# Group 0 of a DLRM tower in two halves: its columns made by TensorE from masked embeddings, its shifted rows copied at once, and W2 turned wholly inside the loop

## What is computed

```python
def _cin_layer(X0, Xi, W, b):          # X0: B x 39 x 16, Xi: B x Fi x 16
    Wr = W.reshape(H, F0_, Fi)         # H = 128
    return jnp.einsum('hjk,bjd,bkd->bhd', Wr, X0, Xi) + b[None, :, None]
...
for W, b in Ws:                        # W0, W1, W2
    Xi = _cin_layer(X0, Xi, W, b)
    res.append(Xi.sum(axis=2))         # z: 512 x 384
h = jnp.maximum(concat([z, dense_ctx]) @ W_top1 + b_top1, 0.0)
h = jnp.maximum(h @ W_top2 + b_top2, 0.0)
y = h @ W_top3
```

## Time and profile before

| what | value |
|---|---|
| median of 3 runs | 670.46 us (669.49 to 670.49) |
| profiled execution, first to last instruction | 667.2 us |
| around the span, by the median | 3.3 us |
| TensorE busy | 642.2 us (96%) |
| VectorE, ScalarE, GpSimd busy | 572.6, 561.4, 358.9 us |
| first layer 1 matmul | at 40.48 us |

### The profile page before, as it was taken

How to read it: one execution, slowest core, us unless ns; L and a number is a source line. 1 busy time by engine, 2 the same in 40 slices (tenths; PEclk the granted TensorE clock), 3 DMA queues, 4 the chain that set the end, 5 groups by cost and what they waited for, 6 DMA issues and landing times.

```text
span 667.2 us, 11319 instructions
## 1 busy us (share of the span) xinstructions
PE 642.2 (96%) x2662; PEld 482.4 (72%) x2662; DVE 572.6 (86%) x894; ACT 561.4 (84%) x1941; POOL 358.9 (54%) x394
## 2 busy tenths in 40 slices
PE   3899999999999999999999999999999999999998
PEld 2667677777777777777777777777777777777874
DVE  3568888989898989899898989898989989899890
ACT  2558889889898989898888889898989898899773
POOL 7648863837565574747383847556474315142700
PEclk9899999999999999999999999999999999999999
DMA  8245614133240505141413324150504140110000
GB/s 292 22 83 130 122 13 104 22 68 58 41 86 13 107 9 114 10 110 15 106 18 74 50 46 79 18 105 7 116 8 112 10 106 6 43 44 1 1 1 0
DMA packets 67523, 39.52 MB, mean 59 GB/s; under 512 B 58791, under 2 KB 61863, under 8 KB 65349
## 3 DMA queue, kind: packets, MB, share of 16 engines
q1 hardware_dynamic: 60463, 37.71, 25.3%
q0 software_dynamic: 5120, 1.29, 2.6%
q10 hardware_dynamic: 1904, 0.15, 0.2%
HBM read 32.80 MB, written 2.40 MB: 53 GB/s over the span
## 4 chain that ended last, share of the span: by engine, by line
PE 82%; DVE 7%; ACT 5%; issue 4%; DMA 2%; DVEq 0%; ACTq 0%; SPq 0%; POOLq 0%
PE yb L992 19%; PE yb L996 18%; PE yb L993 18%; PE p L958 13%; PE pq L969 5%; DVE acc L816 3%; ACT yb L634 3%; DMA gram<-in_L_rec_W_dram 2%; DVE x L822 2%; DVE yb L800 1%; PE yb L1109 1%; PE pq L923 1%; PE p L1054 1%; PE p L1086 1%; PE p L1084 1%
## 5 line engine op out<-in xcount | busy, mean ns | idle before, releaser
L634 ACT ACTIVATE yb<-yb,x0t 128x128 f32<-128x128 f32 x1728 | 467.4, 369 | 57.5 <-PE yb L996 52.5
L816 DVE TENSOR_TENSOR acc<-acc,yb 128x512 f32<-128x512 f32 (+1 forms) x512 | 323.4, 668 | 32.5 <-ACT yb L634 32.2
L992 PE MATMUL yb<-w1h,x1h 128*128 128x512 f32 (+1 forms) x640 | 307.8, 481 | 6.9 <-DVE acc L816 6.0
L996 PE MATMUL yb<-w1h,x1l 128*128 128x512 f32 (+1 forms) x640 | 247.5, 387 | 0.0
L993 PE MATMUL yb<-w1l,x1h 128*128 128x512 f32 (+1 forms) x640 | 247.2, 386 | 0.0
L427 POOL DMA_INDIRECT emb<-in_table_dram,idx x160 | 152.6, 954 | 44.8 <-issue 38.9
L485 POOL TENSOR_TENSOR late<-late,x0r 117x512 f32<-117x512 f32 (+1 forms) x105 | 132.5, 1297 | 79.6 <-DMA late<-x_scratch 79.4
L992 PEld LDWEIGHTS yb<-w1h,x1h 128*128 128x128 f32 x640 | 120.2, 188 | 62.9 <-DVE acc L816 25.1
L993 PEld LDWEIGHTS yb<-w1l,x1h 128*128 128x128 f32 x640 | 120.6, 188 | 45.8 <-issue 24.7
L996 PEld LDWEIGHTS yb<-w1h,x1l 128*128 128x128 f32 x640 | 120.1, 188 | 25.0 <-DVE x1l L771 0.4
L474 POOL TENSOR_TENSOR bdiag<-mask,x0t 128x312 f32<-128x312 f32 x64 | 45.5, 711 | 142.2 <-PE pq L969 138.9
(11 more groups left out here) (108 smaller groups left out, 317.8 us busy)
## 6 DMA issues: line engine op xcount, KB each, us to landing
late<-x_scratch SPq DMA_DIRECT2D x45, 312.0 KB
late<-x_scratch SPq DMA_DIRECT2D x30, 234.0 KB
emb<-in_table_dram,idx POOLq DMA_INDIRECT x160
gram<-in_L_rec_W_dram SPq DMA_DIRECT2D x1, 2496.0 KB, 11.0
x_scratch<-x0r SPq DMA_DIRECT2D x15, 156.0 KB
late<-x_scratch SPq DMA_DIRECT2D x15, 156.0 KB
w2t<-in_L_rec_W_dram SPq DMA_DIRECT2D x1, 1280.0 KB, 14.5
x0t<-embt SPq DMA_DIRECT2D x64, 20.0 KB
```

Of the source, the lines that this page charges most:

```text
L634: op = act.activation(part, part, ACT.Copy, scale=x0t[u][:, t, j:j + 1])
L816: dve.tensor_tensor(part, part, parts(y_bank(t, m), n), ALU.add).then_inc(summed, 1)
L992: pe.matmul(y[:, 0:w], hi, w1h[:, at:at + w], start=True, stop=False)
L996: pe.matmul(y[:, 0:w], lo, w1h[:, at:at + w], start=False, stop=True).then_inc(bank_ready, 1)
```

## The change

Group 0's 32 samples go through the head in two halves of 16 (tiles 0 and 1, tiles 2 and 3). The ids and table offsets are loaded so that one gather brings two fields' columns for 16 samples; the first half needs 5 gathers and not 10. VectorE widens each gathered block by a mask (`widen`), and TensorE makes the columns from it with 10 small matmuls (`half_px`), in the place of `dims_outside`, `samples`, `columns` and `three_times` for this group. ScalarE copies all shifted rows in two instructions (`half_shifts`). VectorE makes W0 symmetric in 4 larger instructions and does pairs in 4. The `WARM` turns are gone. W1 comes in two DMAs. The second half's columns, turns, shifts, pairs and `layer0` are placed in tiles 0 and 1 of period 0. Fields of group 1 are turned at (2, 2) of period 0, of group 2 at (0, 6) and of group 3 at (3, 6) of period 1; layer 0 of group 1 runs from (3, 3) to (3, 9) of period 0, that of group 2 from (1, 9) to (3, 2) of period 1. All ten banks of W2 are turned in the loop. The rows in the DRAM scratch are read with a stride of three rows.

```diff
-FIRST_LAYER0_SLOTS = ((1, 8), (2, 0), (2, 2), (2, 5), (2, 8), (3, 1), (3, 4))
-NEXT_TURN_SLOT, NEXT_COPY_SLOT = (0, 0), (0, 0)
-W2_FIRST = 5
-W2_SLOTS = ((4, 6), (4, 9), (5, 6), (5, 9), (6, 9))
+PX_SLOT, HALF_TURN_SLOT = (0, 5), (0, 8)
+HALF_THREE_SLOT, HALF_COPY_SLOT = (0, 7), (0, 9)
+HALF_SHIFT_SLOTS = ((1, 0), (1, 2), (1, 4), (1, 6))
+HALF_LAYER0_SLOTS = {(1, 3): (0, 1), (1, 5): (2, 3), (1, 7): (4, 5), (1, 8): (6,)}
+HALF_HIGH_SLOT = (1, 9)
+SPREAD_AT, HALF_LOW_AT = (0, ("sum", 1)), (1, ("sum", 7))
+HALF_PAIRS_AT = (("scale", 0), ("sum", 1), ("sum", 4), ("fold before", 0))
+THREE_SLOTS = {0: {(2, 1): 1}, 1: {(0, 4): 2, (3, 0): 3}}
+TURN_SLOTS = {0: {(2, 2): 1}, 1: {(0, 6): 2, (3, 6): 3}}
+COPY_SLOTS = {0: {(2, 2): 1}, 1: {(0, 7): 2, (3, 7): 3}}
+EARLY_LAYER0 = {0: {(3, 3): (0,), (3, 5): (1,), (3, 6): (2,), (3, 8): (3,), (3, 9): (4, 5, 6)},
+                1: {(1, 9): (0,), (2, 1): (1,), (2, 3): (2,), (2, 5): (3,), (2, 8): (4,), (3, 0): (5,), (3, 2): (6,)}}
+HIGH_SLOTS = {0: (3, 9)}
+W2_SLOTS = ((3, 6), (4, 1), (4, 9), (5, 1), (5, 6), (5, 9), (6, 1), (6, 6), (6, 9), (7, 1))
-WARM = 24
...
-                        first = x0d[u, c0 + CHUNKS * q:c0 + CHUNKS * q + FIELDS, :]
+                        first = x0d[u, REPS * c0 + q:REPS * c0 + q + FIELDS, :]
-                        src = bass.AP(first.tensor, first.offset, [[row, FIELDS], [row, n], [1, GROUP_N]])
+                        src = bass.AP(first.tensor, first.offset, [[row, FIELDS], [REPS * row, n], [1, GROUP_N]])
...
+            def half_columns(h):
+                px = pq[:, 0:HALF_T * COLS].rearrange("p (t c) -> p t c", t=HALF_T)
+                tiles = slice(h * HALF_T, (h + 1) * HALF_T)
+                act.wait_ge(px_done, h + 1)
+                act.activation(x0t3[:, tiles, :].rearrange("p t (r j) -> p t r j", r=REPS),
+                               px[:, :, None, 0:FIELDS].to_broadcast([P, HALF_T, REPS, FIELDS]),
+                               ACT.Copy).then_inc(half_x0t3_ready, 1)
+                act.activation(x0t[0][:, tiles, :], px, ACT.Copy).then_inc(half_x0t_ready, 1)
...
+            def half_px(h):
+                if h > 0:
+                    pe.wait_ge(half_x0r_ready, h)
+                for k in range(HALF_K):
+                    pe.wait_ge(wide_ready, h * HALF_K + k + 1)
+                    for t in range(HALF_T):
+                        px = pq[:, t * COLS:(t + 1) * COLS].rearrange("p (q i k) -> p k i q", i=HALF_I, k=HALF_K)
+                        op = pe.matmul(px[:, k], wide[h][:, k, t * P:(t + 1) * P],
+                                       mask[:, :].rearrange("p (i q) -> p i q", i=HALF_I), start=True, stop=True)
+                op.then_inc(px_done, 1)
...
+            for n in range(W0_BANKS):            # TensorE's head
+                turn_w0(n)
+            half_px(0)
+            for b in range(4):
+                turn_w1(b)
+            half_turn(0)
+            half_shift(0, 0)
+            half_shift(0, 1)
+            turn_order = {1: 2, 3: 3}
             for c in range(CHUNKS):
-                layer0(0, c)
+                half_layer0(0, c)
+                if c in turn_order:
+                    half_shift(0, turn_order[c])
+            for b in range(4, W_BANKS):
+                turn_w1(b)
...
             for n in range(W0_BANKS):            # ScalarE's head
+                copy_w0(n)
+            copy_w1(0)
+            half_columns(0)
+            half_shifts(0, 0, 2)
+            half_fields(0)
+            half_shifts(0, 2, CHUNKS)
+            for b in range(1, 4):
+                copy_w1(b)
...
+            half_high(0)
+            for b in range(4, W_BANKS):
+                copy_w1(b)
...
+            for k in range(HALF_K):              # VectorE's head, behind W0
+                widen(k)
+            for b in range(4):
+                low_w1(b)
+            for s in range(DOUBLES):
+                half_products(0, s)
+            low_w1(4)
+            half_low(0)
+            for b in range(5, W_BANKS):
+                low_w1(b)
```

More of the change, by code:

```diff
@@ L199, in tower @@
         w0_in = sem("w0_in")
-        w1_in = sem("w1_in")
+        w1_in = [sem(f"w1_in{h}") for h in range(len(W1_PIECES) - 1)]
         w2_in = [sem(f"w2_in{h}") for h in range(len(W2_PIECES) - 1)]
@@ new lines, in half_shifts @@
+            def half_shifts(h, c0, c1):
+                act.wait_ge(half_x0t3_ready, h + 1)
+                first = x0t3[:, h * HALF_T:(h + 1) * HALF_T, REPS * c0:REPS * c0 + FIELDS]
+                part, tiles, cols = first.ap
+                n = min(REPS * c1, SHIFTS) - REPS * c0
+                act.activation(shifted[h][:, :, REPS * c0 * FIELDS:(REPS * c0 + n) * FIELDS].rearrange("p t (r j) -> p t r j", r=n),
+                               bass.AP(first.tensor, first.offset, [part, tiles, [1, n], cols]),
+                               ACT.Copy).then_inc(half_shifts_ready, 1)
@@ new lines, in half_turn, with half_shift @@
+            def half_turn(h):
+                pe.wait_ge(half_x0t3_ready, h + 1)
+                pe.wait_ge(half_x0t_ready, h + 1)
+                for t in range(HALF_T):
+                    op = pe.transpose(pq[0:ROWS, t * P:(t + 1) * P], x0t3[:, h * HALF_T + t, :], ident[:, :])
+                op.then_inc(half_turned, 1)
+            def half_shift(h, s):
+                if h == 0:
+                    head_bank_free("shift", s)
+                elif s == 0:
+                    pe.wait_ge(x0r_ready, 1)
+                else:
+                    pe.wait_ge(pairs_ready, 2 * s)
+                y = head_bank("shift", s) if h == 0 else pq
+                pe.wait_ge(half_shifts_ready, 2 * h + (1 if s == 0 else 2))
+                for n, c in enumerate(doubles(s)):
+                    rows = chunk_rows(c)
+                    for t in range(HALF_T):
+                        op = pe.transpose(y[0:rows, n * HALF_N + t * P:n * HALF_N + (t + 1) * P],
+                                          shifted[h][:, t, c * ROWS:c * ROWS + rows], ident[:, :])
+                op.then_inc(half_shifted, 1)
@@ new lines, in half_layer0 @@
+            def half_layer0(h, c):
+                rows, cols = chunk_rows(c), half_cols(h)
+                if h > 0 and c == 0:
+                    pe.wait_ge(half_x1h_ready, h)
+                    pe.wait_ge(half_x1l_ready, h)
+                    pe.wait_ge(half_z0_ready, h)
+                if h == 0:
+                    pe.wait_ge(half_pairs, c // 2 + 1)
+                else:
+                    pe.wait_ge(pairs_ready, c + 1)
+                op = pe.matmul(p0[:, cols], w0t[0:rows, c, :], pairs[0:rows, c, cols],
+                               start=(c == 0), stop=(c == CHUNKS - 1))
+                if c == CHUNKS - 1:
+                    op.then_inc(half_l0_done if h < HALVES - 1 else l0_done, 1)
@@ L942, in turn_w2 @@
                 pe.wait_ge(gram_copied, T - 1 if m >= GRAM_AT else T - 2)
[L943 to L945 removed]
+                pe.wait_ge(x0r_ready, turned_before(T, m))
+                if b > 0:
+                    pe.wait_ge(w2_back, b)
                 for j in range(4 * b, min(4 * b + 4, FIELDS)):
@@ L982, in layer1_bank @@
                 k = of.index(m)
+                if isinstance(T, int) and T == 0:
+                    pe.wait_ge(w_hi, W0_BANKS + m + 1)
+                    last = [i for kind, i in HEAD_RING[-RING:] if kind == "w1" and head_bank(kind, i) is y_bank(t, m)]
+                    pe.wait_ge(w_lo, max(last + [m]) + 1)
                 if k >= ring:
```

498 lines of the change are left out of this document (292 added, 206 removed).

## The result

The changed kernel takes 707.7 us (706.9 to 709.5, 4 runs) where the kernel before takes 670.0 on the same chip: 1.057 times as long, interval 1.056 to 1.058. The forecast was 693.0, range 681 to 702. So the direction was right and the time 14.7 us too low, outside the range. The profiled execution has a span of 705.7 us (before 667.2), and the sum on record has to be held against the 38.5 us between them.

What follows compares the result with a forecast made beforehand. TensorE, busy 642 of 667 us, was taken as the bound. Head -9.5, tiles 0 and 1 +12.1, tiles 2 and 3 +6.0, period 1 +6.6, tile 8 +7.7: +22.9 on 667.2, plus 3.3 to the median: 693, range 681 to 702.

Steps and rivals of the forecast that it cites:

- T8: Tile 8, +7.7 us: TensorE waits for group 3's first chunk, whose copy at (3, 7) comes too late.
- Idle time of tiles 2 and 3: Waits within +6.0 us: 1.05 at turn_fields(1) for three_times, 3.55 for group 1's first chunk at (3, 3).
- The trip: Copied x0r through DRAM to its first chunk's start on GpSimd: 9.7 us, bounds 7.5 and 11.2.
- the likeliest case: Whole kernel: the summed stretches with a 9.7 us trip give 693, bounds 687 to 699; chance 0.62.
- rival about the rows' spacing: DRAM read in 2 KB pieces: shorter trip, 7.5 us, gives 686 (0.12); longer, 11.2 us, gives 701 (0.08).
- waits of tiles 0 and 1 do not add: Rival: TensorE runs ahead in the rings, so 8.3 us of waits fall to about 3, giving 688; chance 0.09.
- Not slower: Rival: chunks are there when asked, only TensorE's work counts, 670, at best 668; decided at T8; chance 0.09.
- the clock was counted once: Head, around 21 to 23.4 us: lower clock after TensorE stands still, loss of 1.4 us, range 0 to 3.6.
- The head: Up to the first layer 1 matmul: from 40.5 to 31.0 us, gain 9.5, range 6.5 to 12.
- Period 1: +6.6 us: work 2.2, gram products waiting for W2 copies, and a 2.95 wait for group 2's chunk.
- 0.4 in T6 and T7, that of T5 hidden: Period 1: gram products at m = 3 waiting for W2 copies; T4's such wait was put at 1.1.
- Tiles 0 and 1: From 15.0 to 27.2 us, +12.1: work +3.8 and in-order waits totalling 8.3.

Runs made afterwards that it cites:

- run 1: Changed kernel with group 3's columns, turn and copy six banks earlier and the last W2 turn moved into tile 3: 702.5 us, ratio 1.047.
- run 5: Changed kernel with the rolled read taking neighbouring rows again, not every third: 724.6 us, ratio 1.067, on the chip with the kernel before at 679.3.
- run 2: Changed kernel with the first four layer0 calls of group 1 later, from (3, 6) and not (3, 3): 703.7 us, ratio 1.050.
- run 3: Changed kernel plus unused identity turns, 20 ahead of the first half's layer0 and 24 at (3, 3): 703.6 us, ratio 1.051.
- run 4: Changed kernel with W1's second half and W2's first half loaded only after the fifth gather landed: 706.2 us, ratio 1.055.
- run 12: Changed kernel with five repairs: runs 1, 2, 4, run 3's 20 head turns, and W2's turns moved off the gram products: 689.9 us, ratio 1.031.
- run 15: Run 12's kernel with W2 not turned at all (layer 2 output not the reference's): 692.1 us, ratio 1.033.
- run 11: Changed kernel with W2 not turned (layer 2 output not the reference's): 702.3 us, ratio 1.051, beside the changed kernel's 708.8.
- run 10: Changed kernel with W2's ten banks turned at other places, no copy right ahead of a gram product: 703.0 us, ratio 1.051.
- run 7: Kernel before with all ten banks of W2 turned in the loop, none in the head: 688.5 us, ratio 1.013, on the second chip.
- run 13: Kernel before with all ten banks of W2 turned in the loop, repeat of run 7: 681.3 us, ratio 1.017.
- run 14: Kernel before with all W2 turns in the loop, at places not right ahead of a gram product: 679.1 us, ratio 1.014.
- run 9: The changed kernel itself, unedited, run again as yardstick: 708.8 us, ratio 1.058, kernel before at 669.2.
- run 6: Changed kernel with W2 not turned (layer 2 output not the reference's), first time, on the second chip: 719.0 us, ratio 1.061.
- run 8: Changed kernel with four repairs, runs 1, 2, 4 and run 3's 20 head turns, on the second chip: 712.4 us, ratio 1.049.

## Why the prediction was wrong in size, step by step

**What held.** The mechanism and the order of the stretches: the head gains and every stretch behind it loses more. T8: 7.4 for a forecast of 7.7, released by GpSimd's chunk behind the scratch, and run 1 shows that the slot is the cause. Idle time of tiles 2 and 3: 4.3 for 4.6, in part by luck (2.60 at the chunk for 3.55, 0.49 at the turn for 1.05, the rest in waits that the prediction did not list). Steady periods: as before. The trip: 10.0 to 10.3 us for 9.7, in the likeliest case; neither rival about the rows' spacing was there (run 5). The rival "waits of tiles 0 and 1 do not add" fell: 13.7. "Not slower" fell at T8, as it said.

**The step that failed first: the clock was counted once.** The sum has 1.4 us for it, in the head, and nothing behind other waits, though the earlier trace rows show the price of one wait. Tiles 0 and 1 ran at a mean of 0.94 (28.73 x 0.06 = 1.7 us), tiles 2 and 3 at 0.89 (31.28 x 0.11 = 3.4), and from 155 to 160 us TensorE was busy at 0.54 (5 x 0.46 = 2.3 of the 2.8 found behind T8). By the clock alone that is 7.4 us. But a slower TensorE then waits less for the others, so not all of it moved the end. In run 2 the clock was 1.00 from the head to T8: tiles 0 and 1 took 28.30 us and not 28.73, with waits of 1.01 and 1.85 us where there were 0.43 and 1.47, and T2 took 9.58 and not 10.24 (first bank to T3's first bank). That is 0.4 and 0.7; with the 1.6 at group 1's chunk (run 2; run 3 has 1.5) and the 2.3 behind T8 it makes 5.0 of the 15.6 us by which the sum missed the span. The Trainium skill ("TensorE: Matmul & The Clock Gate", Part 1), cited in the prediction, has the lower clock after idling; the changed kernel's trace agrees at each of these waits, other traces not at all of them (last section), and I applied the rule only where the removed turns had stood.

**The head: 5.9 and not 9.5.** The fifth gather at 16.9, the forecast 13.8, outside its bounds (16.0). I took a rate for 10 KB rows from the earlier trace rows and shared it one for one; the gathers had 53 packets in 3.5 us. Run 4 shows the contention by removing it. What 3.4 us at the gathers are worth at the end of the head depends on the clock: 1.2 in run 4, and 2.0 to 2.5 with the clock at 1.00 (30.18 and 30.59 in runs 12 and 15 against 32.62 and 32.68 in runs 11 and 3).

**Period 1: 11.3 and not 6.6.** The waits behind W2 were put at 1.5. The trace has three gram products at 1.03 each, 1.9 at the two turns of fields (for the copy of a gram product out of the same bank) and 0.9 at turns of W2. The step that failed is "0.4 in T6 and T7, that of T5 hidden". The busy time rose by 5.05 for 2.2 forecast: TensorE's lines have W2's turns at 2.4 more, one more turn of fields 0.7, gram products 0.4; the other 1.5 isn't placed. Run 10 shows the waits (3.7 us of period 1 beside the work that moved), runs 7 and 13 show them in the kernel before. Group 2's chunk, forecast as a wait of 2.95, had 0.60 because W2 had made TensorE late for it; run 11 shows the hand-over (4.62 without W2).

**Tiles 0 and 1: 13.7 for 12.1.** Busy 8.3 more: small matmuls 2.4, turns and shifts 3.1, the half's `layer0` 3.7, less 1.6 for what left, and some 1 us of clock. Idle 5.4, of which 1.98 stands ahead of T2. So the work came out 4.5 us above the 3.8 on record and the waits 2.9 below the 8.3, in part since the small matmuls did not lie under one. That the sum is near is luck: the two errors went against each other. This split is read from the trace; no run took these waits apart.

**What is left.** With five waits repaired, 20.7 us stand above the kernel before. 3.2 are the head against tiles 0 and 1, 6.3 lie in tiles 2 and 3 (to T4's second bank), 8.1 in period 1 and 2.1 at T8 (by the trace, which has 20.1 in all). For the last two run 15 shows that W2's work isn't what bounds: in both traces TensorE waits for the trips of groups 2 and 3. No run took tiles 2 and 3 of this kernel apart, and how much moving group 2's copy sooner would give wasn't tried. No version beat the kernel before.

## What to carry to other kernels

Price a wait of TensorE with its echo: here waits of 2 to 3 us were followed in most traces, not in all, by 3.4 us at half the clock. Where no further wait stood behind, that cost 1.6 to 1.9 us more; where one did, 0.4 to 0.7, as that wait shrank. Turns without use in a wait get the clock back, not the wait; moving the waiting work behind banks gets both. And read more than one trace before a difference of a us or two is put down to an edit. A head that ends sooner is worth nothing if what it leaves out is put in the loop, where the engine has no idle time to cover it: W2 alone cost 11.5 us there. And with one PSUM bank for three users, leave room for the copy between two of them: with two banks between the turn and the next user that one waited 0.9 to 1.4 us (runs 13 and 14), with four (turn at bank 9, gram product at bank 3) no gram product did (run 10). Then look what the saved time runs into next.

## What the runs showed of the hardware

In the changed kernel a block of 20 matmuls of 8 columns (2.37 us) was followed by the lower clock just as a wait was: 0.50 from 44 to 47 us, with TensorE busy 0.79 to 1.00 in each microsecond.

The same place does not always bring the fall. The wait of 1.98 us ahead of T2 stands in all of the undisturbed traces of the changed kernel and its variants (1.97 in two of them). It was followed by a lower clock in seven (the changed kernel, runs 1, 3, 9, 11, 12 and 15) and not in runs 2, 4 and 10. In these three the block of small matmuls brought no fall either, and the low stretch in the head lasted 6.8 us and not 3.4. Run 12's wait of 2.06 us had none behind it. Where T8 waited 7.7 to 8.0 us, the lower clock came each time. What decides it for the short waits, the runs don't show.

Runs 5 to 8 were on a chip where the kernel before took 679.3 us (676.6 to 681.3) in place of 669.2 to 670.0. There engines stood still with nothing in the profile to release them, for up to 9 us. Timelines of VectorE and TensorE in run 8:

```profile
34.21 1.02 DVE L925 TENSOR_TENSOR late<-yb,x0r 117x512 f32<-117x512 f32 x2 [9.19 <-remote]
```

```profile
73.13 0.77 PE L1225 MATMUL yb<-w1h,x1h 128*128 128x512 f32 x1 [6.19 <-issue]
```

The chain of waits of these runs has a share of up to 2% for "another core or an unknown queue", which the other chips' runs lack. The two queues that the profile calls "instruction" moved no packet in either stretch of run 8 (25 to 34.2 and 67 to 73.1 us), so a load of code is not seen there; the cause stays open. What it teaches is to run the changed kernel beside every batch.
